# A two-layer graph network on one core: GpSimd's weight splits in pieces, two hidden chunks taken apart early, and node groups of 2, 4 and 4 tiles

## The reference, cut to what matters

```
h = relu(layernorm(x))
agg = segment_sum(h[src], dst)                       # first layer
z = (1 + eps) * h + agg
h1 = relu(batch_norm(z @ W01 + b1))                  # 512 -> 1024
r  = relu(batch_norm(h1 @ W02 + b2))                 # 1024 -> 512
x = x + h + r
h = relu(layernorm(x))                               # second layer
e = mish(concat(h[src], h[dst], edge_attr) @ W1 + b1)
m = mish(e @ W2 + b2)
agg = segment_sum(m, dst)
u = mish(concat(h, agg) @ W3 + b3)
x = x + layernorm(h + u @ W4 + b4) * gamma + beta
```

## Time and profile before

| | |
|---|---|
| median of 3 runs | 1177.58 us (1175.31 to 1177.83) |
| the profiled execution | 1177.56 us, span 1175.8 us |
| TensorE busy | 1076.2 us, 92% of the span |
| VectorE busy | 888.4 us, 76% |
| ScalarE busy | 899.6 us, 77% |
| GpSimd busy | 672.0 us, 57% |

### The profile page before, as it was taken

The page is one execution under the profiler, slowest core; times in us unless marked ns, Lnnn a source line. Parts: engine busy times, 40 slices in busy tenths (PEclk is TensorE's granted clock), DMA queues, the critical chain, the costliest instruction groups (busy, mean ns, idle before and its releaser), DMA issues.

```text
span 1175.8 us, 18391 instructions
## 1 busy us (share of the span) xinstructions
PE 1076.2 (92%) x5689; PEld 907.3 (77%) x5690; DVE 888.4 (76%) x1493; ACT 899.6 (77%) x1134; POOL 672.0 (57%) x564
## 2 busy tenths in 40 slices
PE   3566998899798889999999999999999999999897
PEld 0112888899587778888888888888888888888695
DVE  7798525453546148888898998989988888888787
ACT  6795843542520479999999999999999999999584
POOL 8696303000314267767788888888876776760117
PEclk7565998999799989999999999999999999999899
DMA  2001920120144367666666666666666666661002
GB/s 99 8 1 55 184 85 0 35 83 1 72 150 128 63 145 153 150 137 133 136 134 142 130 135 141 134 136 140 131 139 138 140 132 132 143 133 44 1 2 87
DMA packets 61087, 121.40 MB, mean 103 GB/s; under 512 B 7851, under 2 KB 18348, under 8 KB 60918
## 3 DMA queue, kind: packets, MB, share of 16 engines
q0 software_dynamic: 38048, 87.58, 36.8%
q1 hardware_dynamic: 22998, 33.32, 8.4%
HBM read 107.82 MB, written 7.80 MB: 98 GB/s over the span
## 4 chain that ended last, share of the span: by engine, by line
PE 83%; DVE 10%; ACT 3%; issue 2%; POOL 1%; DVEq 1%; ACTq 0%; POOLq 0%
PE banks L990 12%; PE banks L985 12%; PE banks L986 12%; PE banks L879 9%; PE banks L970 6%; PE banks L1005 6%; PE banks L964 6%; PE banks L941 5%; PE banks L805 4%; PE banks L922 4%; DVE edge_counts L1601 3%; PE banks L983 3%; DVE key_onehot L1557 2%; PE banks L1051 2%; PE banks L859 1%
## 5 line engine op out<-in xcount | busy, mean ns | idle before, releaser
L646 POOL DMA_INDIRECT gather_pq<-q_table,dst x157 | 299.0, 1904 | 61.9 <-issue 47.5
L638 POOL DMA_INDIRECT gather_pq<-p_table,src x157 | 173.3, 1104 | 159.1 <-PE banks L970 107.0
L985 PE MATMUL banks<-w_lo,h_hi 128*128 128x512 f32 x628 | 245.2, 390 | 0.0
L986 PE MATMUL banks<-w_hi,h_hi 128*128 128x512 f32 x628 | 244.9, 390 | 0.0
L990 PE MATMUL banks<-w_hi,h_lo 128*128 128x512 f32 x628 | 168.4, 390 | 0.0
L1863 DVE SCALAR_TENSOR_TENSOR h_full<-mish_work,banks 128x512 f32<-128x512 f32 (+1 forms) x158 | 100.9, 680 | 51.2 <-ACT mish_work L1274 48.5
L986 PEld LDWEIGHTS banks<-w_hi,h_hi 128*128 128x128 f32 x628 | 118.3, 188 | 25.3
L990 PEld LDWEIGHTS banks<-w_hi,h_lo 128*128 128x128 f32 x628 | 117.9, 188 | 24.5
L985 PEld LDWEIGHTS banks<-w_lo,h_hi 128*128 128x128 f32 x628 | 118.4, 189 | 22.2
L1262 ACT ACTIVATE mish_work<-banks 128x1024 f32<-128x1024 f32 (+1 forms) x79 | 80.6, 1021 | 31.4 <-PE banks L970 31.4
L964 PE MATMUL banks<-ident,gather_pq 128*128 128x128 f32 x628 | 95.8, 275 | 7.6 <-DVE h_full L1863 7.6
(11 more groups left out here) (249 smaller groups left out, 2723.9 us busy)
## 6 DMA issues: line engine op xcount, KB each, us to landing
edge_attr<-in_edge_attr_t SPq DMA_DIRECT2D x79, 128.0 KB
x_nodes<-h_hi POOLq DMA_DIRECT2D x10, 256.0 KB, 12.9
x_nodes<-h_lo POOLq DMA_DIRECT2D x10, 256.0 KB, 7.9
p_table<-p_stage SPq DMA_DIRECT2D x10, 256.0 KB, 2.0
q_table<-agg_nodes SPq DMA_DIRECT2D x10, 256.0 KB
gather_pq<-p_table,src POOLq DMA_INDIRECT x157
gather_pq<-q_table,dst POOLq DMA_INDIRECT x157
x_nodes<-in_x SPq DMA_DIRECT2D x3, 768.0 KB, 6.3
```

What stands on the lines that cost most here:

```text
L638: nc.gpsimd.indirect_dma_start(GP[:, 2 * j + k, :], None, p_tab[:, :], bass.IndirectOffsetOnAxis(ap=SRC[:, 2 * s + k:2 * s + k + 1], axis= ...
L646: nc.gpsimd.indirect_dma_start(GP[:, 2 * j + k, :], None, q_tab[:, :], bass.IndirectOffsetOnAxis(ap=DST[:, 2 * s + k:2 * s + k + 1], axis= ...
L985: pe.matmul(at, H_HI[:, j, c, e], W2_LO[:, c, :], start=False, stop=False)
L986: pe.matmul(at, H_HI[:, j, c, e], W2_HI[:, c, :], start=False, stop=False)
```

## The change

Three edits. The cast and the subtraction of W02 are made in eight pieces of 512 columns each, those of W3's first half in four; all casts come first, then all subtractions, each of which waits for its own cast. The waits of TensorE count the pieces.

Chunks 0 and 1 of `hidden_t` (`HIDDEN_EARLY = 2`) are cast and subtracted during the first product, two output chunks behind the one that is moved. `hidden_hi` puts them into the half of its first place that is free by then. The cast of chunk 2 follows the product's last move on ScalarE, and VectorE subtracts it between the last chunk's statistics and its four tiny operations; the last `apply` now stands behind the cast of chunk 4.

`FILLS` changes from groups of 4, 4 and 2 node tiles to groups of 2, 4 and 4.

```diff
-FILLS = [(a, min(a + 4, NT)) for a in range(0, NT, 4)]
+FILLS = [(0, 2)] + [(a, min(a + 4, NT)) for a in range(2, NT, 4)]
+HIDDEN_EARLY = 2
@@ hidden_hi
-            return H1_HIGHS[k // (KH // 2)][:, k % (KH // 2), :]
+            half = KH // 2
+            return H1_HIGHS[k // half][:, (k + (half - HIDDEN_EARLY if k < half else 0)) % half, :]
@@ gpsimd (the same for W3A with KD pieces)
-            nc.gpsimd.tensor_copy(W02_HI[:, :, :], WB[:, :, :]).then_inc(w02_hi, 1)
-            pool.wait_ge(w02_hi, 1)
-            nc.gpsimd.tensor_tensor(W02_LO[:, :, :], WB[:, :, :], W02_HI[:, :, :].bitcast(F32), ALU.subtract).then_inc(w02_lo, 1)
+            for k in range(KH):
+                nc.gpsimd.tensor_copy(W02_HI[:, k, :], WB[:, k, :]).then_inc(w02_hi, 1)
+            for k in range(KH):
+                pool.wait_ge(w02_hi, k + 1)
+                nc.gpsimd.tensor_tensor(W02_LO[:, k, :], WB[:, k, :], W02_HI[:, k, :].bitcast(F32), ALU.subtract).then_inc(w02_lo, 1)
@@ move_product, after each block's move
+                        if between and b == BLOCKS // 2:
+                            between(o)
@@ scalar
-            last_std, last_apply = move_product(MM_1, H1T, KH, CB1, VAR_BN1, 1)
-            last_std()
-
-            act.wait_ge(mm_done, MM_2)
-            for k in range(KH):
+            def hidden_high(k):
                 act.wait_ge(bn_applied, k + 1)
                 nc.scalar.copy(hidden_hi(k), H1T[:, k, :]).then_inc(h1_hi, 1)
-                if k == 0:
-                    last_apply()
+            def hidden_early(o):
+                if 0 <= o - 2 < HIDDEN_EARLY:
+                    hidden_high(o - 2)
+            last_std, last_apply = move_product(MM_1, H1T, KH, CB1, VAR_BN1, 1, between=hidden_early)
+            act.wait_ge(mm_done, MM_2)
+            hidden_high(HIDDEN_EARLY)
+            last_std()
+            hidden_high(HIDDEN_EARLY + 1)
+            hidden_high(HIDDEN_EARLY + 2)
+            last_apply()
+            for k in range(HIDDEN_EARLY + 3, KH):
+                hidden_high(k)
@@ batch_norm, behind bn_aggr
+                    if behind_last and o == on - 1:
+                        behind_last()
@@ vector
-            batch_norm(H1T, KH, CG1, CBE1, MM_1, VAR_BN1)
-            for k in range(KH):
+            def hidden_low(k):
                 dve.wait_ge(h1_hi, k + 1)
                 nc.vector.tensor_tensor(H1_LO[:, k, :], H1T[:, k, :], hidden_hi(k).bitcast(F32), ALU.subtract).then_inc(h1_lo, 1)
+            def hidden_early(o):
+                if 0 <= o - 2 < HIDDEN_EARLY:
+                    hidden_low(o - 2)
+            batch_norm(H1T, KH, CG1, CBE1, MM_1, VAR_BN1, between=hidden_early, behind_last=lambda: hidden_low(HIDDEN_EARLY))
+            for k in range(HIDDEN_EARLY + 1, KH):
+                hidden_low(k)
```

More of the change, by code:

```diff
@@ L654, in _ @@
             pool.wait_ge(w3a_in, 16)
-            nc.gpsimd.tensor_copy(W3A_HI, WA[:, 0:KD, :]).then_inc(w3a_hi, 1)
-            pool.wait_ge(w3a_hi, 1)
-            nc.gpsimd.tensor_tensor(W3A_LO, WA[:, 0:KD, :], W3A_HI.bitcast(F32), ALU.subtract).then_inc(w3a_lo, 1)
+            for k in range(KD):
+                nc.gpsimd.tensor_copy(W3A_HI[:, k, :], WA[:, k, :]).then_inc(w3a_hi, 1)
+            for k in range(KD):
+                pool.wait_ge(w3a_hi, k + 1)
+                nc.gpsimd.tensor_tensor(W3A_LO[:, k, :], WA[:, k, :], W3A_HI[:, k, :].bitcast(F32), ALU.subtract).then_inc(w3a_lo, 1)
             pool.wait_ge(q_stored, TABLE_STORED)
@@ L904, in _ @@
                       z0_lo, lambda k: Z0_READY[k])
-            pe.wait_ge(w02_lo, 1)
+            pe.wait_ge(w02_lo, KH)
             product_t(MM_2, (W02_HI, W02_LO), (hidden_hi, lambda k: H1_LO[:, k, :]), KH, KD,
@@ L943, in u_terms @@
                 mm.then_inc(mm_done, 1)
-            pe.wait_ge(w3a_lo, 1)
+            pe.wait_ge(w3a_lo, KD)
             pe.wait_ge(mm_moved, FREE + MM_PQ + NT)
@@ L1089, in move_hi_node, with move_product @@
                               TR[:, (base + nt) % 4, :].rearrange("p (c e) -> p c e", c=KD), scale).then_inc(done, 1)
-            def move_product(base, target, on, bias, var, apply_at):
+            def move_product(base, target, on, bias, var, apply_at, between=None):
                 def std(o):
@@ L1222, in normalise_2 @@
             def normalise_2(nt):
-                if nt % 4 == 0:
-                    act.wait_ge(scale_ready, LG + nt // 4 + 1)
+                for g, (a, b) in enumerate(FILLS):
+                    if nt == a:
+                        act.wait_ge(scale_ready, LG + g + 1)
                 nc.scalar.activation(H[:, nt, :], X[:, nt, :], ACT.Relu, bias=NBIAS[:, nt:nt + 1],
@@ L1426, in ln_scale, with batch_norm @@
                                                ALU.mult, ALU.mult).then_inc(scale_ready, 1)
-            def batch_norm(source, on, gamma, beta, base, var, between=None):
+            def batch_norm(source, on, gamma, beta, base, var, between=None, behind_last=None):
                 for o in range(on):
```

## The result

The changed kernel takes 1163.83 us (median of 4 runs, 1163.43 to 1164.72), the kernel before 1176.44 on the same chip (4 runs, 1175.23 to 1177.83): ratio 0.9895, 95% interval 0.9880 to 0.9911. The forecast was 1158.7 with a range of 1155.5 to 1165. The profiled execution took 1164.13 us with a span of 1162.3, 13.5 less than before; the sum of the terms was 18.9.

What follows compares the result with a forecast made beforehand. It took TensorE as the bound, its edge loop full and untouched, so gains lay ahead of that loop. Terms 6.9 + 6.1 + 0.6 + 5.3 = 18.9 us off 1177.56 gave 1158.7 us, range 1155.5 to 1165.

Steps and rivals of the forecast that it cites:

- A: First product: W02 in pieces lets VectorE in between them, ending TensorE's stall; 6.9 us won, bounds 0 and 6.9.
- B: Between first and second product: hidden_t chunks 0 and 1 taken apart early; 6.1 us won, bounds 3.5 and 6.3.
- The drawn chain: Second product under B: chunk 3 0.2 us late, later chunks in time, first block complete 13.0 us after the start.
- Rival 3: Second product: B gives only its two early chunks, 3.5 us instead of 6.1, total 1161.3 us; chance 0.13.
- C: Ahead of the first P product: first group of two tiles starts it earlier; 0.6 us won, bounds +0.6 and -1.2.
- D: Edge tables, q products: W3's first half in pieces removes TensorE's wait for moves; 5.3 us won, bounds 4.3 and 5.3.
- Rival 1: W02 and W3 pieces: VectorE locked out through whole runs; A +2.3, D +0.6, C nothing, B stays, 1174.4 us; chance 0.08.

Runs made afterwards that it cites:

- chained kernel: Changed kernel with every W3 piece waiting for the piece before it, casts first, then subtractions: 1156.86 us, 0.9838 of the kernel before.
- W3 whole: Changed kernel with W3's first half again in one cast and one subtraction: 1163.68 us, 0.9900 of the kernel before.
- pairs: Changed kernel with each W3 cast followed by its own subtraction, which waits for that cast: 1156.16 us, 0.9839 of the kernel before.
- the one with the distance: Changed kernel, GpSimd waiting for node tile 5's move before W3's pieces, with extra VectorE additions in the first layer and edge tables: 1157.79 us, one run.

## Why the prediction was right, and where a step of it failed

**A, right.** 6.84 in the timeline for 6.9, and 6.6 where it alone was undone. The first product takes 56.40 us against 56.3 forecast, the granted clock of 190 to 200 us is 1.00 where it was 0.75, and the longest stand of a one-column operation is 1.22 us.

**B, right.** 5.88 for 6.1, 5.9 where it alone was undone. The drawn chain held: product start to first move of act_t took 13.29 us, for 13.0. Rival 3 (only the two early chunks, 3.5) is refuted.

**C, wrong in sign, and small.** The term said 0.6 won; 0.48 was lost. The prediction named the reason as its bound: the two-input operation in that chain stood for a W1 piece. Rows of VectorE and ScalarE:

```profile
289.18 0.69 DVE L1816 TENSOR_TENSOR x_nodes<-x_nodes,banks 128x512 f32<-128x512 f32 x1 [0.47 <-PE banks L866]
...
289.97 1.22 DVE L1444 SCALAR_TENSOR_TENSOR ln_bias<-ln_mean_var,rstd 128x2 f32<-128x2 f32 x1
...
291.22 1.52 ACT L1244 ACTIVATE h_nodes<-x_nodes,ln_bias,rstd 128x512 f32<-128x512 f32 x2 [2.19 <-DVE ln_bias L1444]
```

The smaller group comes up earlier, while GpSimd's run of four W1 pieces is still on; with the old group the same operation comes at 291.60, behind it, and takes 0.16. What the early start wins, the stand takes back. Only 0.3 of the 0.48 goes with the groups: from apply to P product it is 9.41 us with the old ones, where the kernel before took 9.23. No run tells where the other 0.2 come from.

**D, the step that failed.** "With pieces, L1850 and L1851 wait 0.64, later 1.24, per piece" was the forecast; in the changed kernel L1878 waits 7.81 us for eight pieces. Its bound (shut out through the four casts, tile 5's move late by 1 us) was too narrow, since the subtractions shut VectorE out as well. Rival 1, locked out through a whole run, was right here and wrong in the first layer; it was posed for both places or none. It gave D +0.6; measured is +1.55, of which 1.0 is TensorE's longer wait (4.4 for 3.4: 0.34 from the longer run, 0.6 from the addition behind it, which rival 1 did not count). The rest lies in the matmuls behind it, with a granted clock of 0.86 from 340 to 365 us, where the chained kernel has 1.00. The term itself was well sized: once VectorE gets in, D gives 5.8 to 6.3 us (66.45 against 60.62 and 60.19).

The prediction also set aside the one row that showed what parts pieces. In the kernel before, VectorE got in between a cast and a subtraction with an open wait between them, and the text noted that "after the pieces' casts that wait is long met". For the first layer that didn't matter, for the edge tables it did.

The row that it put on the other side of the scale was misread. It takes L1652's ten subtractions as standing beside GpSimd's src_onehot run, but in the trace of the kernel before only two of them do (starts 51.70 and 59.18 us). The other eight begin at 110.86 or later, and the last src_onehot row ends at 103.27. One of the two:

```profile
59.18 0.68 DVE L1652 TENSOR_TENSOR h_lo<-h_nodes,h_hi 128x512 fp32r<-128x512 f32 x1
```

The two took their 0.68 us with no stand at all beside operations of 0.62 us each, so they say little on what VectorE does at the border between two pieces that do hold it.

The Trainium skill (GPSIMD Engine Reference, section 2.1 Instruction dispatch) says that a core of GpSimd starts the next instruction as soon as its own share of the last is done. The trace agrees in what its rows can show: the four W3 casts end at 343.80 + 2.28 = 346.08 and the first subtraction begins at 346.04; the W02 casts end at 178.59 and the next begins at 178.56. The overlap is the same in both places and VectorE's fate is not, so that rule alone does not forecast it.

**What made up for it.** By the table A fell short by 0.06, B by 0.22, C by 1.08 and D by 6.85, together 8.2 us; 0.25 ahead of the change and 2.55 behind the first u product came back, and 5.4 is left, as 18.9 - 13.5. No term stood for the 2.55. Of it, 0.6 lie between that product and the first exponential, 1.4 between the first exponential and the fifth (408.48 to 434.21 before, 396.93 to 421.26 after). TensorE's granted clock is lower in that stretch before (0.83 over 10 us, some 1.7 us of work at full clock as an estimate) than after (1.00). Windows of before, then of after:

```profile
420.00:430.00 10.00, 7.79 (x36) 6.65 (x36) 3.63 (x5) 5.83 (x8) 7.34 (x6) 0.83 0.70 177
```

```profile
410.00:423.00 13.00, 12.01 (x68) 10.32 (x69) 7.25 (x10) 10.24 (x13) 9.03 (x8) 1.00 0.76 160
```

No run tried this part by itself, but the traces of the experiments show that it is no gain of the change to count on. Behind the first u product all thirteen changed kernels have the same code, and from there to the end of the span nine of them take 798.2 to 798.9 us (the changed kernel 798.4) and four take 799.8 to 800.3 (W3 whole 800.2). The kernel before took 800.9. W3 whole lost 1.8 of its 2.4 us there.

So the total fell into the range because A and B, the larger half, were sized to 0.3 us, and by luck: an uncounted 2.55 us, most of which comes and goes between kernels with the same code, covered a part of D's miss. Without it the changed kernel would stand near 1166.4, above the range.

**What stays open.** Why VectorE is shut out between W3's pieces in the changed kernel is settled only this far. Seven kernels, in all of which the eight pieces follow straight on the gathers with no wait added, show a stand of 5.97 to 7.81 us: the changed one, the three with additions ahead of or in the run, and those with A undone, with B undone and with the old groups. Five show it gone: pairs and chain, each with new and old groups, where gathers are as near but waits stand between the pieces, and the one with the distance (a single run). Whether the gathers' nearness or the missing open wait at the run's start does it would need a run with the wait but with a gather straight ahead of it, or the first layer's run behind a gather. Neither was tried.

## What to carry to other kernels

Cutting a long GpSimd instruction into pieces doesn't by itself let VectorE's two-input operations in. What did wherever it was tried here, in four kernels, was a wait between the pieces on the piece just issued. Add it, and price the turn-taking at about one operation of the other side per piece. Look at each place apart; the same cut freed VectorE in the first layer and locked it out for 7.81 us behind the gathers. And when a small group is brought forward, look at what it now runs beside: 0.6 us of an earlier start went into one stand of 1.22 us.

## What was not expected of the hardware

- An addition of one column stood 7.28 us and one of 512 columns 7.81 us, each to the end of eight GpSimd instructions: the time shut out does not depend on the width.
- With turns taken, 512-wide pieces go from 0.57 to at most 1.10 us (casts, in the pairs) and from 1.24 to 1.62 (subtractions; 6.82 / 4 = 1.71 in the run with the distance), and the kernels are still 6 to 7.7 us quicker than the changed one by the medians, since the first W3 product comes earlier all the same (355.85 and 356.19 for 363.93).
- In the two rows on C above L1816, one of whose inputs is in PSUM, took its 0.69 us in the midst of W1's pieces, and L1444, with both inputs in SBUF, stood 1.22 there although it has two columns.
